# Second attention of a two-layer kernel: maxima of its first group of heads made in the stage before it

## The reference

```python
kv_d, q_d = x @ kv_d_w, x @ q_d_w                 # latents
k_p, q_p, v = kv_d @ k_u_w, q_d @ q_u_w, kv_d @ v_u_w
k_r, q_r = rope(x @ rope_k_w), rope(q_d @ rope_q_w)
k, q = concat(k_p, k_r), concat(q_p, q_r)
scores = einsum('bhqd,bkhd->bhqk', q, k) * scale   # causal mask, then softmax
out = einsum('bhqk,bkhd->bqhd', softmax(scores), v) @ o_w
```

## Time and profile before

| | us |
|---|---|
| median of 3 runs | 1911.91 |
| lowest, highest run | 1907.4, 1913.23 |
| time of the profiled execution | 1912.08 |
| its span in the trace | 1910.4 |
| busy TensorE, VectorE, ScalarE, GpSimd | 1689.1, 1467.5, 1234.5, 697.7 |

### The profile page before, as it was taken

One profiled execution on the slowest core, in us unless ns is written; L12 is line 12 of the kernel. 1 busy time (PEld: TensorE's weight loads), 2 busy tenths in 40 slices (PEclk: granted clock), 3 DMA queues, 4 the chain that ended last, 5 costly groups with the idle time before them and its releaser, 6 DMA issues. The chain is left out here.

```text
span 1910.4 us, 31941 instructions
## 1 busy us (share of the span) xinstructions
PE 1689.1 (88%) x10554; PEld 1172.0 (61%) x10554; DVE 1467.5 (77%) x3080; ACT 1234.5 (65%) x2769; POOL 697.7 (37%) x1326
## 2 busy tenths in 40 slices
PE   4979899999999878788889998888876899987998
PEld 3547644444444467667668876776754545545887
DVE  6767689999998267999997869999446788916654
ACT  2534377887778533789886768888752688865222
POOL 2002212222222214666665646666232111125532
PEclk9989899999999899888889999889987799987999
DMA  3364122233320200000000000000037222110001
GB/s 121 116 215 89 34 54 55 62 68 68 68 60 10 75 1 1 1 1 1 1 1 1 1 1 1 1 1 1 1 115 186 43 56 56 35 74 1 1 1 45
DMA packets 36132, 82.27 MB, mean 43 GB/s; under 512 B 9856, under 2 KB 11776, under 8 KB 34944
## 3 DMA queue, kind: packets, MB, share of 16 engines
q1 hardware_dynamic: 35968, 80.22, 16.8%
HBM read 52.53 MB, written 27.26 MB: 42 GB/s over the span
## 5 line engine op out<-in xcount | busy, mean ns | idle before, releaser
L1140 ACT ACTIVATE probs<-pss 128x512 f32<-128x512 f32 (+3 forms) x1152 | 481.8, 496 | 129.0 <-PE pss L1103 127.9
L848 DVE TENSOR_REDUCE negmax<-px 128x2 f32<-128x1024 f32 (+2 forms) x480 | 508.5, 1113 | 45.5 <-PE px L830 42.6
L1697 POOL TENSOR_SCALAR rp<-sw,tau 128x256 f32<-128x256 f32 x720 | 341.8, 507 | 7.1
L1207 POOL TENSOR_SCALAR_AFFINE_SELECT probs<-probs 128x512 f32<-128x512 f32 x192 | 120.4, 635 | 506.8 <-ACT probs L1140 506.8
L1103 PE MATMUL pss<-queries,keys 64*128 64x512 f32 (+3 forms) x1152 | 295.9, 396 | 5.5 <-ACT probs L1140 4.3
L830 PE MATMUL px<-keys,queries 63*128 63x512 f32 (+3 forms) x1152 | 266.8, 420 | 10.5 <-DVE negmax L848 10.5
L1103 PEld LDWEIGHTS pss<-queries,keys 64*128 64x128 f32 x1152 | 167.6, 190 | 152.3 <-ACT probs L1140 134.5
L1117 PE MATMUL po<-probs,vals 128*32 128x512 f32 (+3 forms) x2304 | 248.7, 508 | 0.4 <-POOL probs L1207 0.2
L1546 PE MATMUL pss<-again,sw 128*128 128x256 f32 x1024 | 247.0, 400 | 0.0
L1851 DVE BATCH_NORM_STATS2 st<-rp 128x6 f32<-128x512 f32 x360 | 229.7, 675 | 2.3 <-POOL rp L1697 2.3
L1546 PEld LDWEIGHTS pss<-again,sw 128*128 128x128 f32 x1024 | 205.5, 205 | 29.3
(11 more groups left out here) (375 smaller groups left out, 2587.1 us busy)
## 6 DMA issues: line engine op xcount, KB each, us to landing
queries<-rec_q SPq DMA_DIRECT2D x96, 128.0 KB, 3.4
keys<-rec_k SPq DMA_DIRECT2D x96, 128.0 KB, 3.5
queries<-rec_q SPq DMA_DIRECT2D x96, 64.0 KB, 3.4
keys<-rec_k SPq DMA_DIRECT2D x96, 64.0 KB, 3.4
rec_q<-fs SPq DMA_DIRECT2D x16, 256.0 KB, 4.4
rec_k<-fs SPq DMA_DIRECT2D x16, 256.0 KB, 4.9
rec_q<-vals SPq DMA_DIRECT2D x16, 256.0 KB, 3.1
rec_k<-vals SPq DMA_DIRECT2D x16, 256.0 KB, 3.6
```

The lines of the kernel that those rows point to most:

```text
L848: return e.tensor_reduce(out, from_px, X_AXIS, ALU.max, negate=True)
L1140: e.activation(tl.probs[arg][:, w, :], tl.pss[scores % 3][:, 512 - width:512], ACT.Exp).then_inc(self.exp_made, 1)
L1697: x = e.tensor_scalar(self.rp[rp % 6][:, :, h], self.view(g, q)[:, h, :], -BIG, self.tau[r][:, 2 * q + h:2 * q + h + 1], ALU.min, ALU.max)
```

## The change

Group 0's 20 passes, the turn, the copy and the row DMA of the second attention move into block 3 of `LatentProjections`, by the class `FirstMaxima`. The pair `px` takes the two banks of `pt`, whose tiles are now views of it. Six passes (EARLY) stand between the queries and plain keys of block 3 and its rotated keys. The other fourteen follow the last `values`; on VectorE seven of them (BESIDE) stand ahead of the rest of TURNED_K and seven behind it. SP sends the rows after the loads of groups 1 and 2. The 1-kind case of `row` leaves out the subtraction, as `Attention` does.

```diff
--- before.py
+++ after.py
@@ -587,6 +587,7 @@
             self.pg, self.pu = [k.ps("pg", [P, 512]) for _ in range(2)], [k.ps("pu", [P, 512]) for _ in range(2)]
             self.py = [k.ps("py", [P, D]) for _ in range(2)]
             first.px = k.ps("px", [P, 2, 512])
+            first.negmax = k.sb("negmax", [P, 2, 4, QT])
             self.sg = [k.sb("sg", [P, 512]) for _ in range(2)]
             self.fz = [k.sb("fz", [P, 512]) for _ in range(3)]
             self.fh, self.fl = ([k.sb(n, [P, 512], F32R) for _ in range(self.SLOTS)] for n in ("fh", "fl"))
@@ -859,7 +860,7 @@
     def __init__(self, k):
         self.k, self.ops = k, None
         self.units = [(w, chunk) for chunk in Attention.CHUNKS for w in (0, 2)]
-        self.negmax, self.rows = k.sb("negmax", [P, 2, 4, QT]), k.sb("rows", [4 * QT, P], F32R)
+        self.rows, self.negmax = k.sb("rows", [4 * QT, P], F32R), None
         self.x_in, self.x_read, self.steps, self.whole, self.sent = k.sems("x_in x_read steps whole sent")
         self.px = None
 
@@ -885,7 +886,11 @@
 
         most, n = self.negmax, len(self.units)
         e.wait_ge(self.x_read, n)
-        e.tensor_tensor(most[:, 0, :, 4:QT], most[:, 0, :, 4:QT], most[:, 1, :, 0:4], ALU.min).then_inc(self.steps, 1)
+        least = e.tensor_tensor(most[:, 0, :, 4:QT], most[:, 0, :, 4:QT], most[:, 1, :, 0:4], ALU.min)
+        if self.ops.nk == 1:
+            least.then_inc(self.whole, 1)
+            return
+        least.then_inc(self.steps, 1)
         e.wait_ge(self.steps, 1)
         e.tensor_tensor(most[:, 0, 3::-2, :], most[:, 0, 3::-2, :], most[:, 0, 0:3:2, :],
                         ALU.subtract).then_inc(self.whole, 1)
@@ -1925,9 +1930,10 @@
     PARTS = ((0, 0), (1, 0), (0, HD // 2), (1, HD // 2))
     SCALES = (HD ** -0.5, 1.0, HD ** -0.5, 1.0)
     stores_go_on = True
-
-    def __init__(self, k, operands, place):
-        self.k, self.operands = k, operands
+    EARLY, BESIDE = 6, 7
+
+    def __init__(self, k, operands, place, first):
+        self.k, self.operands, self.first = k, operands, first
         self.vals = k.vals
 
         self.names = (("wd", [P, DC, P]), ("lat", [P, 2 * D]), ("xk", [P, DC, D]))
@@ -1941,7 +1947,9 @@
             self.xh, self.xl = ([k.sb(n, [P, DC, 512], F32R) for _ in range(2)] for n in ("xh", "xl"))
             self.dh, self.dl = ([k.sb(n, [P, 512], F32R) for _ in range(2)] for n in ("dh", "dl"))
             self.ta, self.tb = ([k.sb(n, [P, 512]) for _ in range(2)] for n in ("ta", "tb"))
-            self.pt = [k.ps("pt", [P, DC, P]) for _ in range(2)]
+            first.ops, first.negmax, first.px = operands, k.sb("negmax", [P, 2, 4, QT]), k.ps("px", [P, 2, 512])
+
+            self.pt = [first.px[:, n, 0:DC * P].rearrange("p (c q) -> p c q", c=DC) for n in range(2)]
             self.pd = k.ps("pd", [P, 512])
             self.pa, self.pb = [k.ps("pa", [P, 512]) for _ in range(2)], [k.ps("pb", [P, 512]) for _ in range(2)]
             self.pv = k.ps("pv", [P, D])
@@ -1984,6 +1992,7 @@
         for g in range(1, ops.early):
             e.wait_ge(self.cleared, 2 * (g + 1))
             ops.load(k, e, g)
+        self.first.send(e)
 
     def wait_stored(self, e):
         for n in range(4):
@@ -2095,11 +2104,17 @@
             queries_and_plain_keys(i, lambda: turn(4 * i + 6) if more else None)
             if more:
                 turn(4 * i + 7)
+            if not more:
+                for n in range(self.EARLY):
+                    self.first.product(e, n)
             turned_k(i)
             values(i, 2)
             if more:
                 latents(i + 1)
             values(i, 3)
+        for n in range(self.EARLY, len(self.first.units)):
+            self.first.product(e, n)
+        self.first.turn(e)
 
     def act(self, e):
         k = self.k
@@ -2232,6 +2247,9 @@
             rest(i, self.PLAIN_K)
             if more:
                 low(4 * i + 6)
+            else:
+                for n in range(self.EARLY):
+                    self.first.largest(e, n)
             turned(i, 0)
             if more:
                 low(4 * i + 7)
@@ -2239,7 +2257,13 @@
             rest(i, self.TURNED_Q)
             if more:
                 latents(i + 1)
+        for n in range(self.EARLY, self.EARLY + self.BESIDE):
+            self.first.largest(e, n)
         rest(NB - 1, self.TURNED_K)
+        for n in range(self.EARLY + self.BESIDE, len(self.first.units)):
+            self.first.largest(e, n)
+        self.first.row(e)
+        self.first.copy(e)
 
     def pool(self, e):
         ops = self.operands
@@ -2659,10 +2683,11 @@
     with k.scope() as layer:
         k.vals = k.sb("vals", [P, NT, H, 32])
         operands = AttentionOperands(k, ["std"], layer, 3)
-        latents = LatentProjections(k, operands, half)
+        second = FirstMaxima(k)
+        latents = LatentProjections(k, operands, half, second)
         out.append(latents)
         with k.scope():
-            out += [Attention(k, operands, AttentionTiles(k, operands), latents)]
+            out += [Attention(k, operands, AttentionTiles(k, operands), latents, second)]
     with k.scope():
         k.xh, k.xl = k.sb("xh", [P, DC, T], F32R), k.sb("xl", [P, DC, T], F32R)
         out.append(OutputAndExperts(k))
```

## The result

| | median | runs | ratio to before |
|---|---|---|---|
| before | 1912.57 | 4, 1907.4 to 1915.73 | |
| changed | 1931.49 | 4, 1928.44 to 1936.61 | 1.0113, 95% interval 1.0095 to 1.0131 |

The change makes the kernel slower: the medians lie 18.9 us apart, and the ratio 1.0113, taken from the same runs but not as the quotient of the medians (1.0099), stands for 21.6 us. The profiled execution took 1930.97 us, with a span of 1929.2.

What follows compares the result with a forecast made beforehand. Before the first scores, group 0's 20 passes ran at VectorE's pace; moved, they alternate on one pair and delay SP's queue. Scores 20.4 us later on 1912.08 profiled gave 1932.5, median 1932; range 1928 to 1937, low end extended to 1924.

Steps and rivals of the forecast that it cites:

- What a pass costs: Block 3, group 0's passes on one `px`: product plus reduction plus two handoffs, 1.62 to 2.30 us by width.
- the sum: Pass costs added over group 0's 20 passes: 40.8 us where 22.5 stood; 18.3 more expected with one pair.
- Where they fall: Block 3: early passes from 1454.50, rotated keys from 1464.98, last reduction ends 1500.8, row chain ends 1502.0 instead of 1463.4.
- What is late next: SP's queue: last store 23.4 us later, rows issued at 1503.2 behind loads, scores at 1509.7, 20.4 us later.
- Served in turn: Row DMA behind SP's loads: rows wait out 5.5 us of transfers, giving 20.4 us; 16.0 if a small DMA passes.
- The 1.0 us for the rows' own part: Row DMA's own time behind the backlog: taken as 1.0, the middle between nothing and 2.04 us.
- The clock: TensorE in block 3: products taken at 1.2 GHz, with PEclk 0.50 from 1470 on.
- The rival with 2.4 GHz: TensorE through block 3's passes: products 0.30 us shorter, 6.3 us saved in all, +14.1, so 1926; chance 0.14.
- Behind the start: Second attention from its first scores on: unchanged, costed at nothing, 2 us either way for when the clock rises.

Runs made afterwards that it cites:

- woven kernel: Changed kernel with two bank pairs from the second pass, two rotated-key matmuls between passes, rotation's first half ahead of the passes on VectorE: 1909.26 against 1910.61, ratio 0.9987.
- kernel woven one by one: As the woven kernel, but one rotated-key matmul between passes 2 to 13, values and rotation's second half later, SP's loads inside block 3: 1909.19 against 1906.45, ratio 1.0013.

## Why the prediction was right

The forecast of 1932 stands against 1931.49. The mechanism is the one forecast, but that the two agree to 0.5 us is in part luck: in the profiled execution the first scores came 21.1 us later than before, not 20.4 (1.1 of that ahead of the change), and 2.3 us came back behind them, where the forecast had nothing. The steps:

- **What a pass costs.** Predicted 1.62, 2.30, 1.82, 2.19 and 2.11 by width; measured 1.62, 2.25, 1.83, 2.20 and 2.12. The kernel before with one pair confirms the sum: 18.0 where the sum gave 18.3.
- **Where they fall.** Rotated keys predicted at 1464.98, measured 1465.69; the last reduction at 1500.8, measured 1501.48; end of the copy at 1502.0, measured 1502.69. All are some 0.7 late, and the block itself started 1.1 late, so within the block they are 0.4 early. That the early passes fill hardly any idle time was implied by the sum, which put passes and rotated keys end to end but for the sixth reduction; the kernel without them bears it out, to about 1.5 us. The rest of TURNED_K cost the chain nothing, as forecast: the reductions on either side of it start 2.12 us apart.
- **What is late next.** Last store predicted at 1486.8, measured 1487.26; row DMA issued at 1503.2, measured 1504.04; its way to the scores 6.5, measured 6.42. Served in turn, as the Trainium skill's rule on ring order in "DMA: Bandwidth & Descriptors", section on queues, rings and completion order, would have it: the trace agrees, with 6.38 us behind a backlog and 2.05 without one. The 1.0 us for the rows' own part fits but is not measured by itself: the DMA engines' share falls to 0.48 in 1509.0 to 1509.5 and 0.13 in the half microsecond behind it, and the rows land at 1510.42.
- **The clock.** It was 0.50 through the late passes but for a rise from about 1470 to 1474 (0.93), at the end of the rotated keys; the 384-wide passes behind it still stood 1.82 us apart. The rival with 2.4 GHz did not come true in this execution. In two of the experiments such a rise lasted longer and was worth 1.2 and 1.5 us, not 6.3.
- **Behind the start.** Costed at nothing. From the first scores to the end the changed kernel took 418.7 us, before 421.1; 1.1 of the 2.3 lie in the first group (from the scores to the copy of group 1's rows 27.4 against 28.5), where the clock rose sooner after the start. The rest was not followed up. The 2.3 us are a little more than the 2 us that were allowed.

The loss has two parts. Up to the copy it is 14.4 us, from the passes; the other 5.6 are the queue. The two kernels with the loads or the row DMA moved show this: they lose 12.9 and 13.2 us (49.4 and 49.7 against 36.5), which is the 14.4 less what the higher clock gave them. The 14.4 come, to 0.1, from three parts: 18.0 for the single pair, less 9.8 us by which the first pass starts earlier (10.64 and 0.81 after the start of the count), plus 6.3 for the rotated keys and values that now stand between the passes, from 1465.69 to 1471.97. Smaller terms cancel in this: 1.0 us less, since the sixth reduction runs beside the rotated keys, and about as much more, mostly since 1.54 us and not 0.9 went from the first pass's start to its reduction, its products running among the last matmuls of the plain keys.

## What to carry to other kernels

Work that is moved ahead into idle time must bring its buffers along: a 512-wide pass that cost 1.13 us on two pairs cost 2.12 on one (18 us over the 20 passes), and the early start was worth less than that. Before moving a wait, ask what stands behind the engine in each queue it passes: here the store that became late held 32 loads, and they held a 16 KB transfer on which everything waited. Idle time of one engine is no room if the work needs two engines in turn and the second one's own work is pushed back by it.

## What the runs showed of the hardware

TensorE's higher clock did not come in every stretch in which it was busy without a gap. Before the change it rose to 2.4 GHz at about 1458.6, within the rotated keys' twelve matmuls, which begin at 1454.66 (first two windows below). In the woven kernel TensorE was busy 13.89 of 14.00 us from 1456 to 1470, with the same twelve matmuls between passes, and the granted clock stayed at 0.50. In the kernel woven one by one it was at 0.50 from 1460 to 1474, with 14.00 of 14.00 us busy (third window).

```profile
1454.60:1458.60 4.00, 3.94 (x9) 3.14 (x10) 1.80 (x3) 0.98 (x2) 1.27 (x1) 0.50 0.96 331
1458.60:1461.20 2.60, 2.12 (x10) 1.26 (x8) 1.29 (x2) 0.38 (x1) 0.78 (x1) 0.97 0.02 6
1460.00:1474.00 14.00, 14.00 (x70) 6.72 (x68) 10.38 (x11) 0.63 (x1) 0.48 (x1) 0.50 1.04 207
```

In all eight traces in which the twelve matmuls stand in a row, the clock rose before the value rows behind them were done; in the two woven ones it did not. What decides it was not tested.
